# A two-layer graph network on one core: weight products regrouped over the couples, and register words biased and masked

## What is computed

```python
# N = 6250 nodes, D = 256, E = 100000 edges sorted by dst, R = 8 relations
def _rgcn_conv(x, W, Wroot, b, src, dst, etype):
    seg = dst * R + etype
    sums = segment_sum(x[src], seg, N * R)
    cnt = segment_sum(ones, seg, N * R)
    mean = (sums / maximum(cnt, 1)).reshape(N, R, D)
    return x @ Wroot + b + einsum('nrd,rde->ne', mean, W)
x = x + conv2(relu(conv1(layernorm(x))))
# then a top-2 mixture of 8 experts, D -> 1024 -> D with GELU, added to x
```

## Time and profile before

| | us |
|---|---|
| median of 3 runs (3499.16 to 3519.07) | 3500.47 |
| span of the profiled execution | 3064.4 |
| outside the span (median less span) | 436.1 |
| first layer's tiles, about | 95 to 1192 |
| second layer's tiles, about | 1207 to 2281 |
| experts, about | 2450 to 3064 |

### The profile page before, as it was taken

How to read it: one execution, slowest core, us unless ns; L and a number is a source line. 1 busy time by engine, 2 the same in 40 slices (tenths; PEclk the granted TensorE clock), 3 DMA queues, 4 the chain that set the end, 5 groups by cost and what they waited for, 6 DMA issues and landing times.

```text
span 3064.4 us, 82720 instructions
## 1 busy us (share of the span) xinstructions
PE 2352.2 (77%) x19212; PEld 1776.0 (58%) x19213; DVE 1782.2 (58%) x4944; ACT 1167.6 (38%) x2306; POOL 1836.5 (60%) x1908
## 2 busy tenths in 40 slices
PE   1456777778888887456777888888987189999999
PEld 0123444555666775123445556667776178888888
DVE  7434445555566664333445555656666278877777
ACT  5001223334445553011223344455542165655554
POOL 1777777766666553777777777666536623333333
PEclk9556789999999998557899999999995599999999
DMA  7343333333333321333343444333335432322222
GB/s 244 100 130 105 108 108 108 109 101 99 97 94 93 90 88 58 106 99 115 115 119 118 123 122 125 112 113 111 106 110 192 146 123 86 100 72 72 72 72 61
DMA packets 164416, 331.14 MB, mean 108 GB/s; under 512 B 35518, under 2 KB 101786, under 8 KB 164216
## 3 DMA queue, kind: packets, MB, share of 16 engines
q0 software_dynamic: 90864, 245.38, 26.9%
q1 hardware_dynamic: 39608, 41.02, 4.5%
q10 hardware_dynamic: 33872, 43.92, 4.5%
HBM read 283.29 MB, written 49.07 MB: 108 GB/s over the span
## 4 chain that ended last, share of the span: by engine, by line
PE 48%; POOL 24%; issue 15%; DVE 7%; DMA 3%; DVEq 2%; ACT 1%; POOLq 0%; SPq 0%; ACTq 0%
POOL ring L450 20%; PE more_banks L1254 15%; PE sum_banks L1392 8%; PE sum_banks L1234 7%; PE sum_banks L1235 5%; PE sum_banks L1382 4%; PE more_banks L1382 4%; POOL lot_in L470 3%; PE more_banks L1246 3%; DMA ring<-table,row_tab 2%; DVE sel L890 1%; DMA out<-edge_work,lot_ids 1%; PE more_banks L1366 1%; DVEq L881 1%; DVE weights L1072 0%
## 5 line engine op out<-in xcount | busy, mean ns | idle before, releaser
L450 POOL DMA_INDIRECT ring<-table,row_tab x1568 | 1509.2, 963 | 703.8 <-issue 339.0
L1254 PE MATMUL more_banks<-weights,stage 128*128 128x256 f16 x5292 | 846.9, 283 | 7.8 <-ACT stage L561 4.5
L589 ACT ACTIVATE stage<-sum_banks,inv 128x256 f16<-128x256 f32 x784 | 327.4, 471 | 815.5 <-DVE inv L923 398.7
L1254 PEld LDWEIGHTS more_banks<-weights,stage 128*128 128x128 f16 x5292 | 502.4, 101 | 144.9 <-issue 71.6
L1234 PE MATMUL sum_banks<-ring,sel 128*128 x1568 | 449.3, 287 | 161.1 <-DVE sel L890 84.2
L898 DVE TENSOR_SCALAR sel_more<-lane,win_off,key_tab 128x128 f16 x780 | 268.8, 345 | 443.4 <-SPq L355 371.2
L1234 PE MATMUL sum_banks<-ring,sel_more 128*128 x780 | 244.3, 314 | 350.0 <-DVE sel_more L898 193.8
L890 DVE SCALAR_TENSOR_TENSOR sel<-lane,win_off,key_tab 128x256 f16<-128x256 f16 x792 | 349.4, 482 | 240.4 <-PE more_banks L1254 235.8
L1235 PE MATMUL sum_banks<-ring,sel 128*128 x1568 | 448.7, 287 | 0.0
L561 ACT ACTIVATE stage<-more_banks 128x1024 f16<-128x1024 f16 x392 | 402.7, 1027 | 15.1 <-PE more_banks L1246 14.9
L1234 PEld LDWEIGHTS sum_banks<-ring,sel_more 128*128 x780 | 78.4, 100 | 529.7 <-issue 524.9
(11 more groups left out here) (287 smaller groups left out, 2763.0 us busy)
## 6 DMA issues: line engine op xcount, KB each, us to landing
ring<-table,row_tab POOLq DMA_INDIRECT x1568
weights<-L_ffn_W ACTq DMA_DIRECT2D x96, 178.5 KB
stage<-L_ffn_W ACTq DMA_DIRECT2D x16, 1024.0 KB, 5.5
edge_work<-lot_in SPq DMA_DIRECT2D x54, 260.0 KB, 2.7
table<-edge_work SPq DMA_DIRECT2D x7, 896.0 KB, 4.4
table<-edge_work ACTq DMA_DIRECT2D x49, 128.0 KB
out<-acc SPq DMA_DIRECT2D x6, 1024.0 KB
acc<-x SPq DMA_DIRECT2D x6, 896.0 KB, 11.0
```

The source lines that it names most:

```text
L450: pool.indirect_dma_start(ring_rows[:, b % RING, 0:2 * D], None, tables[layer], bass.IndirectOffsetOnAxis(row_tab[:, b:b + 1], 0)).then_in ...
L589: act.activation(mean16[:, slot, h, 0:D], ps_sum[slot][h][:, 0:D], ACT.Copy, scale=inv[:, ds(c * 2 + h, 1)]).then_inc(mean_high[layer], 1)
L1254: return [pe.matmul(ps_out[par], rows[:, xp * KD + k, :], w16[:, wp, k, r * D:(r + 1) * D], start=part == 0 and n == 0, stop=part == PARTS ...
```

## The change

1. **Products.** Before, couples k = 0, 1, 2, 3 issue 5, 2, 6, 5 of the 18 products: a tile's products begin behind the sums of the next tile's couple k = 1, where PE waits for `means_in`, and end in the following tile's k = 0. Now they issue 5, 4, 4, 5: a tile's products begin in the next tile's k = 2 (the wait stands ahead of its blocks) and end in the following tile's k = 1. The two root products come first. In k = 1 the products were all behind the blocks; now they stand between them.
2. **Results.** `sums_out` moves from k = 1 to k = 2 on DVE, the bias addition of layer 0 (L944) from k = 2 to k = 1, `relu_rows` on ACT from the end of k = 2 to k = 3 ahead of `turned`.
3. **Registers.** The table holds `lo + 2` (`need`). PE waits for `need & MASK` in place of `lo + 2`. The ring slot of block b is (b + 2) mod 16. In the loop on further blocks the selection's slot is (need + i) mod 16 and the ring's slot (need + i + 2) mod 16, where one value served both, and the value waited for is masked first. SP's and DVE's waits on register values are masked too.
4. **The layer's end.** The last tile but one has 5 products, then the turn, then 4 more. The last tile's two root products stand ahead of the last wait for `means_in`.
5. `lot_meta` holds 16-bit words.

```diff
+    MASK = (1 << (BLOCKS + 3 * WINDOWS).bit_length()) - 1
...
+    PART_ORDER = [R * KD + k for k in range(KD)] + list(range(R * KD))
+    SHARES = (5, 4, 4, 5)
+    SPREAD = {4: (1, 1, 0, 1, 1), 5: (1, 1, 1, 1, 1)}
+    CUTS = (0, SHARES[2], SHARES[2] + SHARES[3], SHARES[2] + SHARES[3] + SHARES[0], PARTS)
...
-        lot_meta = sb("lot_meta", [1, X + 1, 4], i32)
+        lot_meta = sb("lot_meta", [1, X + 1, 4], u16)
...
-                        sp.wait_ge(steps_done[layer], sp.snap(regs[s], donate=True, min_val=1, max_val=BLOCKS + 3 * WINDOWS))
+                        sp.wait_ge(steps_done[layer], sp.snap(regs[s], donate=True) & MASK)
...
-                    pool.indirect_dma_start(ring_rows[:, b % RING, 0:2 * D], None, tables[layer],
+                    pool.indirect_dma_start(ring_rows[:, (b + 2) % RING, 0:2 * D], None, tables[layer],
...
+                        if layer == 0 and k == 3 and age == 2:
+                            relu_rows(t - 2, par)
                         if age > 0 or k > 0:
...
-                            if k == 2 and age == 2:
-                                relu_rows(t - 2, par)
...
-            v.tensor_copy(meta[0:1, 0:WINDOWS, 0], lo)
+            v.tensor_scalar(meta[0:1, 0:WINDOWS, 0], lo, 2.0, None, ALU.add)
...
-                lo = [v.snap(regs[2 * k], donate=True, min_val=0, max_val=BLOCKS - 1) for k in range(count)]
+                lo = [v.snap(regs[2 * k], donate=True, min_val=2, max_val=BLOCKS + 1) - 2 for k in range(count)]
...
-                        v.wait_ge(rows_ready[layer], block + 1)
+                        v.wait_ge(rows_ready[layer], (lo & MASK) + i + 3)
...
-                        if k == 1 and age == 2:
+                        if k == 2 and age == 2:
                             sums_out(t - 2, par)
...
-                            if k == 2:
+                            if k == 1:
                                 here = flat(acc[:, ds(t, 1), :])
...
-                def more_sums(to, lo, since, upto):
+                def more_sums(to, need, since, upto):
                     with pe.If(upto > since):
                         with pe.Fori(0, upto - since) as i:
-                            pe.wait_ge(more_ready[layer], since + i + 1)
-                            block = (lo + i + 2).with_bounds(min_val=0, max_val=BLOCKS - 1)
-                            add_block(to, flat(sel_more[:, ds(block & (RING - 1), 1), :]), block, False, True).then_inc(steps_done[layer], 1)
+                            pe.wait_ge(more_ready[layer], (since & MASK) + i + 1)
+                            add_block(to, flat(sel_more[:, ds((need + i) & (RING - 1), 1), :]), need + i + 2, False, True).then_inc(steps_done[layer], 1)
...
-                    if k == 0:
-                        parts = [(par, n) for n in range(PARTS - 5, PARTS)] if age == 2 else []
-                    else:
-                        parts = [(1 - par, n) for n in (range(0, 2), range(2, 8), range(8, 13))[k - 1]] if age > 0 else []
-                    spread = ((1, 1, 1, 1, 1), (0, 0, 0, 0, 2), (1, 1, 1, 1, 2), (1, 1, 1, 1, 1))[k]
+                    due = (k + 2) % STEPS
+                    of, enough = (par, age == 2) if k < 2 else (1 - par, age > 0)
+                    parts = [(of, n) for n in PART_ORDER[CUTS[due]:CUTS[due + 1]]] if enough else []
+                    spread = SPREAD[SHARES[k]]
...
+                    if k == 2 and age > 0:
+                        if age == 1:
+                            pe.wait_ge(w_split, layer + 1)
+                        pe.wait_ge(means_in[layer], t * STEPS)
...
-                        pe.wait_ge(rows_ready[layer], lo[j] + 2)
+                        pe.wait_ge(rows_ready[layer], need[j] & MASK)
...
-                    if k == 1 and age > 0:
-                        if age == 1:
-                            pe.wait_ge(w_split, layer + 1)
-                        pe.wait_ge(means_in[layer], t * STEPS)
...
-                for n in range(PARTS - 5, PARTS):
+                for n in PART_ORDER[CUTS[2]:CUTS[3]]:
+                    product(1, n)
+                turn(COUPLES - 1, 1)
+                for n in PART_ORDER[CUTS[3]:]:
                     ins = product(1, n)[-1]
                 ins.then_inc(out_done[layer], 1)
-                turn(COUPLES - 1, 1)
+                for n in PART_ORDER[:KD]:
+                    product(0, n)
                 pe.wait_ge(means_in[layer], COUPLES)
```

More of the change, by code:

```diff
@@ L1227, in load_meta, with add_block @@
                 pe.load(regs, meta_row[0:1, ds(2 * w, 2 * WPT + 4)])
-                lo = [pe.snap(regs[2 * k], donate=True, min_val=0, max_val=BLOCKS - 1) for k in range(WPT)]
-                return regs, lo, [pe.snap(regs[2 * k + 1], donate=True, min_val=0, max_val=BLOCKS) for k in range(WPT + 1)]
+                need = [pe.snap(regs[2 * k], donate=True) for k in range(WPT)]
+                return regs, need, [pe.snap(regs[2 * k + 1], donate=True, min_val=0, max_val=BLOCKS) for k in range(WPT + 1)]
             for layer in range(2):
-                def add_block(to, hot, block, first, last):
-                    slot = ring_rows[:, ds(block & (RING - 1), 1), :]
+                def add_block(to, hot, at, first, last):
+                    slot = ring_rows[:, ds(at & (RING - 1), 1), :]
                     pe.matmul(to[:, 0:D + 1], hot, flat(slot[:, :, D:2 * D + 1]), start=first, stop=last, skip_group_check=True)
                     return pe.matmul(to[:, 0:D], hot, flat(slot[:, :, 0:D]), start=False, stop=last, skip_group_check=True)
-                def more_sums(to, lo, since, upto):
+                def more_sums(to, need, since, upto):
                     with pe.If(upto > since):
                         with pe.Fori(0, upto - since) as i:
-                            pe.wait_ge(more_ready[layer], since + i + 1)
-                            block = (lo + i + 2).with_bounds(min_val=0, max_val=BLOCKS - 1)
-                            add_block(to, flat(sel_more[:, ds(block & (RING - 1), 1), :]), block, False, True).then_inc(steps_done[layer], 1)
+                            pe.wait_ge(more_ready[layer], (since & MASK) + i + 1)
+                            add_block(to, flat(sel_more[:, ds((need + i) & (RING - 1), 1), :]), need + i + 2, False, True).then_inc(steps_done[layer], 1)
                 def turn(c, slot):
@@ L1254, in product, with couple @@
                     return [pe.matmul(ps_out[par], rows[:, xp * KD + k, :], w16[:, wp, k, r * D:(r + 1) * D],
-                                      start=part == 0 and n == 0, stop=part == PARTS - 1 and n == 2, skip_group_check=True)
+                                      start=part == PART_ORDER[0] and n == 0, stop=part == PART_ORDER[-1] and n == 2, skip_group_check=True)
                             for n, (xp, wp) in enumerate(PART_PAIRS)]
-                def couple(t, par, age, k, lo, mark):
+                def couple(t, par, age, k, need, mark):
                     c, slot = t * STEPS + k, k % 2
-                    if k == 0:
-                        parts = [(par, n) for n in range(PARTS - 5, PARTS)] if age == 2 else []
-                    else:
-                        parts = [(1 - par, n) for n in (range(0, 2), range(2, 8), range(8, 13))[k - 1]] if age > 0 else []
-                    spread = ((1, 1, 1, 1, 1), (0, 0, 0, 0, 2), (1, 1, 1, 1, 2), (1, 1, 1, 1, 1))[k]
+                    due = (k + 2) % STEPS
+                    of, enough = (par, age == 2) if k < 2 else (1 - par, age > 0)
+                    parts = [(of, n) for n in PART_ORDER[CUTS[due]:CUTS[due + 1]]] if enough else []
+                    spread = SPREAD[SHARES[k]]
                     first = []
@@ L1277, in couple @@
                         to = ps_sum[slot][h]
-                        pe.wait_ge(rows_ready[layer], lo[j] + 2)
+                        pe.wait_ge(rows_ready[layer], need[j] & MASK)
                         if h == 0:
                             pe.wait_ge(sel_ready[layer], c + 1)
-                        add_block(to, sel[:, slot, h, 0, :], lo[j], True, False).then_inc(steps_done[layer], 1)
+                        add_block(to, sel[:, slot, h, 0, :], need[j], True, False).then_inc(steps_done[layer], 1)
                         some(3 * h)
-                        add_block(to, sel[:, slot, h, 1, :], lo[j] + 1, False, True).then_inc(steps_done[layer], 1)
+                        add_block(to, sel[:, slot, h, 1, :], need[j] + 1, False, True).then_inc(steps_done[layer], 1)
                         if h == 0:
                             some(1)
-                        more_sums(to, lo[j], mark[j], mark[j + 1])
+                        more_sums(to, need[j], mark[j], mark[j + 1])
                         if h == 0:
@@ L1304, in tile_work @@
                 def tile_work(t, par, age):
-                    regs, lo, mark = load_meta(t * WPT)
+                    regs, need, mark = load_meta(t * WPT)
                     for k in range(STEPS):
```

(4 more changed lines are left out.)

5 lines of the change are left out of this document (3 added, 2 removed).

## The result

The changed kernel took 3610.3 us (median of 4 runs, 3606.7 to 3615.0) beside 3508.1 us for the one before in the same session (4 runs, 3499.2 to 3519.1): ratio 1.029, 95% interval 1.0265 to 1.0319, 102 us slower. The forecast was 3548 us (+48) with a range from 3450 to 3610, so the measured time lies just above its end. Its side was right; its size was less than half of what was measured.

The account below looks back on a forecast made before the run. PE's sequencer was taken to bound late tiles, gathers the first 11. Products and waits -43 us, registers +92, sum +49 taken as +48: median 3500.5 to 3548 us, range 3450 to 3610.

Parts of the forecast that it names:

- The sequencer of PE sets the pace: Late tiles: PE's sequencer needs 12.9 us per tile, the array 11.4; a loop turn costs 1.10 us.
- the rule that I set beside it: PE's loop: further instructions are queued while sequencer code executes; spoke for the rival of waits alone, 3457 us, chance 0.20.
- The loop's turn, +0.2 us: PE's loop on further blocks: two operations more, 0.2 us per turn, 390 turns per layer.
- The rival of three operations: PE's loop on further blocks: three operations more, 0.3 us per turn, +127 us, 3627 us; chance 0.13.
- The gathers' cover of 32 us per layer: First 11 tiles: gathers exceed PE's sequencer by 32 us per layer, subtracted from the longer turns' cost.
- The late tiles: Late tiles should follow each other every 13.1 to 13.3 us in both layers.
- The products' move, -43 us: Waits holding PE's sequencer before the products shrink: -31 us in layer 0, -12 in layer 1.
- The wait for `mean_low`: Rival: it holds PE's sequencer in place of `means_in`; 43 us more, likeliest 3591 us; no chance of its own given.
- The first 335 gathers 15 to 30 us longer: POOL's early gathers: their stretch grows by 15 to 30 us in each layer.
- The 436 us around the span: 436.1 us of the median lie outside the profiled span of 3064.4 us and stay unchanged.
- "Nothing" for the rest of the registers: Outside PE's loop: `need & MASK`, SP's instruction per block and DVE's one or two in its loop add no time.

Follow-up runs that it names:

- e7: Changed kernel with one index for both rings and the wait's masked number named ahead of PE's loop (still worked out inside it): 3588.6 us, ratio 1.022.
- e9: Changed kernel with PE's loop short: masked number put in a register once per window, one index for both rings: 3505.2 us, ratio 1.011.
- e17: The anchor with PE counting its used masks in its own register, nothing added per window: 3519.2 us, ratio 1.0013.
- e14: The anchor with SP's mask removed and SP's table held as 16-bit words instead: 3611.2 us, ratio 1.0275.
- e3: Kernel before with the change's registers and masks, products where they were: 3248.2 us, ratio 1.060.
- e4: Changed kernel with one index for both rings, VectorE's further selections shifted by two slots to match: 3156.3 us, ratio 1.030.
- e11: Changed kernel with PE's and VectorE's loops both short, masks and moved products kept: 3498.5 us, ratio 1.010.
- e12: e11 with products, results and relu where they were before: 3539.7 us, ratio 1.022.
- e8: e7 with products, results and relu where they were before: 3636.6 us, ratio 1.035.
- e1: Kernel before with its three register tables as 16-bit words, no other edit: 3476.0 us, ratio 1.134.
- e2: e1 with products, results and relu moved as in the change: 3458.9 us, ratio 1.128.
- e10: Changed kernel with VectorE's loop alone made short, PE's turn left at eleven instructions: 3585.5 us, ratio 1.034.
- e15: e11 repeated as the anchor in a later session: 3538.2 us, ratio 1.006.
- e16: The unaltered change, run beside the anchor: 3615.0 us, ratio 1.029.
- the anchor: Changed kernel with PE's and VectorE's loops both short, the code of e11, repeated as e15: 3538.2 us, ratio 1.006.
- e13: The anchor with three SP register instructions per block in place of one: 3537.2 us, ratio 1.007.
- e5: The changed kernel unaltered, run again beside the kernel before: 3613.2 us, ratio 1.029.

## Why the forecast was right on the side and wrong on the size

Its steps one by one, each against what was measured.

- **The sequencer of PE sets the pace**: shown for the loop. Instructions taken out of it bring time (e7, e9), and so do those taken from ahead of it (e17); tripled ones on SP and a shorter loop on VectorE bring none. It is not alone: the longer load on SP cost 73 us (e14). Against the rule that I set beside it, that further instructions are queued while the sequencer's code runs, a turn with the same two matmuls went from 1.10 to 1.39 us.
- **The loop's turn, +0.2 us: mis-sized, the first step that failed.** It is +0.29 to +0.3 (e3). It counted a second AND for the slots, which the turn before already had the earlier trace rows, an addition of its own and the AND of the wait's number, and took two of these three. It lacked the MOVE in front of that last AND. So there are three instructions more, if not the three that were counted: the AND, its MOVE and the addition. The rival of three operations had the right turn; that its 3627 us stands near the 3610 measured is luck, since the prices of the timed runs were others (below). I argued it down with a mask that "may be dropped"; none was.
- **The gathers' cover of 32 us per layer**: about right. With 0.3 us a turn the working gives 2 x (117 - 32) = 170 us for the registers. e3 measured 182 on the quiet chip, with 16 us hidden in layer 0 and about 40 in layer 1. For the registers alone the forecast's method, given the right turn, is good to 12 us there. With the moved products it isn't: for e4 it gives +49 and +90 was measured. Some 20 of these 41 us are the products' term, 5 the experts; the rest is open.
- **The late tiles**: 13.1 to 13.3 us were expected. Over the last ten tiles before has 14.1 us in layer 0 and 13.6 in layer 1, e4 on the quiet chip 13.6 in both: the move pays in layer 0 and hardly in layer 1. Shorter windows of e4 give 80.5 / 6 = 13.4 and 25.9 / 2 = 13.0:

```profile
L1233 PEldq TENSOR_LOAD <-meta x7: 1357/1360/1365, 1139.7 to 1220.2; - x7
...
L1233 PEldq TENSOR_LOAD <-meta x3: 1358/1361/1377, 2307.2 to 2333.1; - x3
```

- **The products' move, -43 us**: 41 us (e11, e12) and 48 us (e7, e8) on the chips of the timed runs, as forecast. On the quiet chip, whose trace the term was read from, it is half: 17 us with the dear loads (e1, e2) and 22 as estimated from e3 and e4. So that it came out in the timed runs is in part luck. The wait for `mean_low` did not take its place.
- **The first 335 gathers 15 to 30 us longer**: the 336th gather starts at 504.2 us before and at 556.5 in e3, 52 us later, and 25 us later counted from the start of layer 1. 15 to 30 us were expected in each layer; layer 0 is above that, layer 1 within.
- **The 436 us around the span, "taken as given": wrong in kind.** They lie inside the span of the runs that were timed. So the sum was made against a trace in which a register instruction costs PE 0.1 us each and the timed runs had another price list: 0.03 to 0.05 us per instruction removed from PE (e7, e9 against e10, e15 against e16; 0.033 is the net figure of e17), about half of the 182 / 2340 = 0.078 us of the quiet chip. That an instruction is partly hidden by stalls that other reasons cause would explain it, but is not shown. The change itself was not run on the quiet chip; e4's 90 us and 70 for one instruction more give 160 us, an estimate, more than three times the forecast for the trace that it was made on.
- **"Nothing" for the rest of the registers: wrong, the second step that failed.** In the timed runs PE's loop and what stood ahead of it in the anchor account for 76.8 + 25.5 = 102 us of the change (two sessions added), the products for -41 to -48. The sum of the two is 54 to 61 us, close to the 48 us forecast, but by luck, since two errors cancel in it: three instructions in place of two, at half the price. What was measured for the whole change is 102 us. The 41 to 48 us between is e17's distance from what it should be, the term that I put at zero.

Of that term the runs all but exclude SP's masks (e13), and exclude the length of VectorE's loop (e9, e11) and the two instructions per window (e17). A small part is the longer load of the experts' words: from the end of the layers' tiles to the end of the span e3 and e4 take 3 to 5 us more than before. Another is e17's turn of 1.2 us for 1.1: 780 x 0.08 = 60 us at the most, 20 to 30 at the prices of these chips, an estimate. Whether the shifted ring or VectorE's instructions per window bring the rest is open; no run moved them alone, and the kernel before has no trace on such a chip beside which to lay one. Nor is it known what a mask costs there in kernels that have no loop on PE.

## What to carry to other kernels

When an engine's sequencer sets the pace, count every register instruction of a loop's body as it will be issued, the copies too: here an AND didn't fuse, and the operand of one that was still in use was copied first. Count the turn before in the same way, too, from its records. What is the same in every turn belongs in a register that is written once, and that it left the loop is seen in the count of records, not in the source. Compare the profiled run's own time with its span before anything is called overhead: if the span is hundreds of us short of the timed runs, trace and times describe two different machines, and the sum should be made for both.

## What the runs showed of the hardware that I had not expected

- **Loads of 16-bit words.** 20 words into PE's registers: 1.36 us as 32-bit, 4.7 to 5.1 us as 16-bit; DVE 1.36 and 4.6; SP's 16 words 0.97 and 3.25. That is 0.20 to 0.25 us per 16-bit word and 0.06 to 0.07 per 32-bit word. The Trainium skill (Runtime: NRT & Kernel Launch, section Instruction fetch mechanics) gives some 200 ns per register, even in bulk, for loads of registers, which it describes as coming from HBM. The tables here stand in SBUF: the 16-bit ones come out near that figure, the 32-bit ones three times as fast.
- **Stalls of 0.7 us on single register instructions**, on PE, VectorE and SP, often near the same moment. In e5, 499.5 to 501.2 us, two on PE back to back and two on VectorE beside them (ns):

```profile
L1240 PEldq FUSED_REGOPS  x2: 702/704/705, 499.8 to 500.5; - x2
...
L938 DVEq ALU_OP  x1: 692/692/692, 499.8 to 499.8; - x1
...
L923 DVEq ALU_OP  x1: 705/705/705, 500.5 to 500.5; - x1
```

  They come in bursts, 85 of some 180 of them 9.5 to 16 us after the burst before and 84 on more than one engine (in the changed kernel's trace), mostly in the early tiles of each layer, on four chips of the experiments, and in no trace of the quiet one, with the same code (e4 and e7). The same page of the Trainium skill says that a taken branch out of the fetched window waits for its instructions to be fetched. The traces speak against it as the cause: these two engines stall together on plain operations in the middle of a body, the same branches cost nothing on the quiet chip, and in the first 700 us of layer 0 of the changed kernel, where 218 such stalls start, only 14 packets fetch instructions:

```profile
q8 instruction: 7, 0.11, 0.1%
q14 instruction: 7, 0.06, 0.0%
```

  e4 and e7 have the same 7 and 7 in that stretch; e4 has no stall in it, e7 has 261. The cause is open.
- **More stalls need not mean more time.** e17 has 319 on PE against 279 in the changed kernel and is 2.7% faster by the ratios; e13's SP has nearly five times the anchor's and the time is the same.
